# Scores of a unit in one PSUM bank, centring moved by two units, and scores moved ahead of the values, in a two-layer attention and FFN kernel

## The chip, the cores and the metric

The kernel runs on one core of a Trainium2 chip. The metric is the device time of one execution in microseconds. The median of three runs of the kernel before is 612.4 us.

## What is computed

Sixteen sequences of 128 tokens with 128 features pass two layers. Each layer is multi-query attention (16 heads of 64, one key and one value head, one null key in front, causal mask, key mask, bias), and after it a feed-forward part; the result is added to x. Layer 1's FFN is dense with ternary weights; layer 2's is a mixture of 8 experts, top 2, capacity 320.

```python
q = (ln(x) @ Wq).reshape(b, n, 16, 64)            # layer 1: l2norm(q), l2norm(k), times 8
k, v = split(ln(x) @ Wkv)                         # null key and value from cond_64 in front
sim = einsum(q, k) + bias                         # layer 1: bias from a small network
attn = softmax(where(causal | masked, -max, sim)) # layer 2: bias is an input, key mask
x = x + ffn(ln(einsum(attn, v) @ Wout, g_out))    # layer 2: routed experts
```

## The kernel before

All matmuls are in float32. The work is written engine by engine, with semaphores by hand. A batch is one sequence; `b` counts the 16 batches of a layer, `B` those of both layers, and `i` is `b % 2`. The 128 queries of a batch are cut into four units `u` of 32 queries; since the mask is causal, unit u needs only 33, 65, 97 or 129 keys (`WIDTH`, the null key included). Heads lie as four groups (h, e), so that one unit's scores are four blocks of 128 x WIDTH[u].

In this text layer 1 and layer 2 are the code's layer 0 and 1. Per batch of layer 2 the queues hold, in program order:

- TensorE (`attention_second`): scores of unit 0 (L855); transposes of unit 2's probabilities of the batch before (L873); values of the pair, units 0 and 1 of the batch before (L881, L882); scores of unit 1; transposes of unit 3 of the batch before; output projection of b - 2 (L910); scores of unit 2; values of units 2 and 3 (L891); input transpose (L801); scores of unit 3; transposes of the pair (L862, L864); keys and values (L819, L821) and queries (L828) of b + 2.
- VectorE: for each unit `biased` (L1547) reads the scores from PSUM, adds the masked bias and takes the maximum; `divide` (L1555, L1559) normalises the unit before; `outputs` (L1571) copies the values from `psO` to `OT`. In unit 0 then follow `centre` of b - 3 (L1608, L1610) and `input_norm` of b + 2 (L1498); in unit 1 `rescale` of b - 3 (L1615); in unit 2 the statistics and copy of the projection of b - 2 and `moments`; in unit 3 `variance` of b - 2 (L1604). `centre` and `rescale` exist from b = 3 on. Routing work stands in b = 10, 11, 14 and 15.
- ScalarE: exponentials (L1255) and the copies of the transposed probabilities to `PT` (L1268, L1262), of keys, queries and inputs.
- Pool: the four bias additions of the next batch (L630), the value subtraction (L613), and `output_rstd` (L577) of b - 2, which waits for `variance`.

Layer 1's queues interleave the same steps in another order; there unit 3 is read in the next batch, and ScalarE also takes squares of the queries for their norms (L1224).

The scores lie in `psS`, two PSUM banks of 512 columns. Head half h of every unit is in bank h. So the scores of a unit wait for the reads of all units before it (`scores_ready`, four for each unit):

```python
apart(pe, ..., (s["scores_ready"], 4 * n))
for h in range(2):
    m = pe.matmul(psS[:, h, 0:2 * w], qT[i][:, h, u].rearrange("p m q -> p (m q)"),
                  kk[i][:, :, 0:w], start=True, stop=True)
```

`over` unrolls the first and last batches of a layer and loops over the rest. `apart` issues waits, the values in registers where they depend on the loop.

Of the kernel before, what the change touches and what calls it, by code (L numbers as in the profile page):

```python
# [54 lines left out]
UNITS = P // QB  # L55
# [13 lines left out]
def build(nc, a, out):  # L69
    ctx = ExitStack()  # L70
    with ctx:
# [250 lines left out]

        def unit_psum(u):
            return psS[:, :, 0:2 * WIDTH[u]].rearrange("p h (e k) -> p h e k", e=2)

# [430 lines left out]
        def _(pe):  # L756
# [88 lines left out]
            def scores(layer, b, u, i):  # L845
                B = b + NB * layer
                n = 4 * B + u
                w = WIDTH[u]
                if no(b, 0) and u == 0:
                    pe.wait_ge(s["kk_null"], 4 * (layer + 1))  # L850

                apart(pe, *([(s["kk_ready"], B + 1), (s["q_ready"], 2 * B + 2)] if u == 0 else []),
                      (s["scores_ready"], 4 * n))
                for h in range(2):
                    m = pe.matmul(psS[:, h, 0:2 * w], qT[i][:, h, u].rearrange("p m q -> p (m q)"),  # L855
                                  kk[i][:, :, 0:w], start=True, stop=True)
# [136 lines left out]
            def attention_second():  # L993
                def batch(b, i):
# [3 lines left out]
                    for u in range(UNITS):  # L998
                        scores(1, b, u, i)
                        if u < 2 and not first:  # L1000
                            turn_probs(B - 1, u + 2, 1 - i)
                        if u == 0 and not first:
                            values_pair(B - 1, 1 - i)
                        if u == 1 and not first and not no(b, 1):
                            project(1, b - 2, i, not last)
# [411 lines left out]
        def _(dve):  # L1417
# [125 lines left out]
            def biased(n, u, i):  # L1543
                apart(dve, (s["probs_ready"], n - 3), (s["bias_ready"], n + 1), (s["scores_psum"], n + 1))
                for g in range(4):
                    h, e = g // 2, g % 2
                    dve.tensor_tensor_reduce(sc[u][:, h, e, :], unit_psum(u)[:, h, e, :], unit_masked(i, u)[:, h, e, :],  # L1547
                                             -1.0, -FAR, ALU.add, ALU.min,
                                             accum_out=negmax[:, u, g:g + 1]).then_inc(s["scores_ready"], 1)
# [201 lines left out]
            def attention_second():  # L1751
                def batch(b, i):
# [4 lines left out]
                    for u in range(UNITS):  # L1757
# [12 lines left out]
                        if u == 2 and not first and not no(b, 1):  # L1770
                            moments(B - 2, i)
                        if u == 0 and normed_now:
                            centre(b - 3, 1 - i)
                        if u == 0 and not last and not no(b, NB - 2):
                            input_norm(1, b + 2, i)
                        if u == 3 and not first and not no(b, 1):
                            variance(b - 2, i)
                        if u == 1 and normed_now:
                            rescale(b - 3, 1 - i)
# [249 lines left out]
```

## Time and profile before

| | |
|---|---|
| median of 3 runs | 612.4 us (610.82 to 613.22) |
| the profiled execution | 614.04 us, span 612.3 us |
| TensorE busy | 491.3 us (80%) |
| VectorE busy | 433.2 us (71%) |
| ScalarE busy | 377.9 us (62%) |
| Pool busy | 310.9 us (51%) |
| scores on TensorE, L855 | 512 instructions, 104.7 us |
| `biased` on VectorE, L1547 | 512, 93.6 us, idle before them 29.6 us |
| granted TensorE clock | mean 0.931 of full speed, 1.00 in most of both attention layers |

Layer 1's attention lies from about 21 to 216 us, the dense FFN to 285, layer 2's attention to about 480, the rest of the routing to 500, the experts to 577, and the gathering of the results behind. Busy time is that of one execution; matmul ends are modelled, so what a TensorE step costs is best read from start to start, where nothing is awaited. Behind a row, in brackets, stands the idle time of its engine before it and who ended it.

### The profile page before, as it was taken

To read this page: it belongs to the slowest core of one execution; us is meant where nothing else is said; L and a number is where in the kernel's file an instruction comes from. 1 tells how busy PE (TensorE), PEld (TensorE's weight loads), DVE (VectorE), ACT (ScalarE), POOL (GpSimd) and SP (SyncE) were. 2 spreads that over 40 slices of the span, in tenths; PEclk is the share of its full clock that TensorE was granted. 3 is DMA by queue.
4 is the path that set the end of the run, shared out by engine and by line. 5 is a ranking of instruction groups with operands and counts; after the bars stand their busy time and mean duration, and the time that the engine had idled before them with its cause. 6 is when DMAs were issued, how large, how long until landed. Compare 5 with 4: busy or idle time off the path is not lost.

```text
span 612.3 us, 13755 instructions
## 1 busy us (share of the span) xinstructions
PE 491.3 (80%) x3220; PEld 395.2 (65%) x3220; DVE 433.2 (71%) x2148; ACT 377.9 (62%) x1475; POOL 310.9 (51%) x368
## 2 busy tenths in 40 slices
PE   3678999999999877948898998988978419999920
PEld 1456777777777655647787887867756307878720
DVE  4899999999999775554778898899797603343403
ACT  1677898888888655634878778767775003443510
POOL 4576666655656517664433343344755531545560
PEclk9789999999999899978899999999998758999975
DMA  5450028331000000000021120000101021222117
GB/s 171 104 151 19 21 60 140 90 97 54 6 8 6 6 1 1 1 0 8 5 77 40 42 75 4 8 6 10 40 26 36 33 74 31 70 61 74 42 34 210
DMA packets 54696, 29.73 MB, mean 49 GB/s; under 512 B 19884, under 2 KB 51572, under 8 KB 54644
## 3 DMA queue, kind: packets, MB, share of 16 engines
q1 hardware_dynamic: 48900, 22.09, 14.6%
q0 software_dynamic: 2560, 4.90, 2.5%
q10 hardware_dynamic: 3184, 2.16, 1.1%
q8 instruction: 18, 0.29, 0.2%
q14 instruction: 34, 0.28, 0.2%
HBM read 16.13 MB, written 10.90 MB: 44 GB/s over the span
## 4 chain that ended last, share of the span: by engine, by line
PE 45%; DVE 20%; issue 14%; POOL 7%; DMA 5%; ACT 4%; SPq 1%; DVEq 1%; another core or an unknown queue 1%; ACTq 0%; POOLq 0%
PE psS L855 9%; PE psS L1152 5%; DVE sc L1547 5%; PE psA L910 4%; PE psO L891 4%; PE psQ L828 4%; PE psQ L812 3%; PE psQ L1142 3%; PE psT L873 2%; DVE centred L1610 2%; DVE OT L1571 2%; POOL wide_buf L630 2%; PE psA L1142 1%; PE psO L1142 1%; ACT qT L1238 1%
## 5 line engine op out<-in xcount | busy, mean ns | idle before, releaser
L1255 ACT ACTIVATE sc<-sc,negmax 128x97 f32<-128x97 f32 (+3 forms) x512 | 179.0, 354 | 34.0 <-DVE negmax L1547 32.2
L855 PE MATMUL psS<-kk,qT 128*128 128x194 f32 (+3 forms) x512 | 104.7, 327 | 23.9 <-DVE negmax L1547 22.2
L1547 DVE CUSTOM_DVE_ANT_0 sc<-psS,wide_buf 128x97 f32<-128x97 f32 (+3 forms) x512 | 93.6, 238 | 29.6 <-PE psS L855 26.6
L630 POOL TENSOR_TENSOR wide_buf<-bias,mask 128x132 f32<-128x132 f32 (+3 forms) x128 | 109.5, 881 | 9.8 <-DVE negmax L1547 4.2
L855 PEld LDWEIGHTS psS<-kk,qT 128*128 128x128 f32 x512 | 79.0, 195 | 50.3 <-issue 47.5
L1255 ACT ACTIVATION_READ_ACCUMULATOR sc<-sc,negmax 128x1 f32 x512 | 97.4, 190 | 0.0
L577 POOL TENSOR_TENSOR qrn<-qssc,half 128x9 f32<-128x9 f32 (+1 forms) x32 | 55.8, 1745 | 59.1 <-DVE qssc L1533 59.1
L1559 DVE TENSOR_TENSOR pn<-sc,rsum 128x128 f32<-128x128 f32 (+3 forms) x128 | 71.7, 560 | 6.8 <-DVE rsum L1555 0.2
L910 PE MATMUL psA<-Wo,OT 128*128 128x128 f32 (+1 forms) x512 | 65.2, 281 | 1.7 <-DVE OT L1571 1.7
L910 PEld LDWEIGHTS psA<-Wo,OT 128*128 128x128 f32 x512 | 62.1, 195 | 2.5 <-DVE OT L1571 2.5
L1571 DVE TENSOR_SCALAR OT<-psO,cols 128x512 f32<-128x512 f32 x64 | 47.6, 744 | 2.7 <-PE psO L891 1.8
L1268 ACT COPY PT<-psT 96x512 f32<-96x512 f32 x64 | 37.0, 577 | 15.8 <-PE psT L873 9.9
L873 PE MATMUL psT<-ident,pn 128*96 128x128 f32 (+1 forms) x256 | 39.6, 278 | 6.0 <-issue 4.1
L1547 DVE DVE_READ_ACCUMULATOR2_ANT negmax<- 128x1 f32 x512 | 41.6, 81 | 0.4 <-issue 0.2
L748 POOL DMA_INDIRECT choice_rows<-hT,tags x24 | 22.5, 939 | 37.1 <-ACT hT L1398 24.5
L891 PE MATMUL psO<-PT,vp 96*64 96x256 f32 (+1 forms) x256 | 34.8, 390 | 7.9 <-DVE OT L1571 4.3
L873 PEld LDWEIGHTS psT<-ident,pn 128*96 128x96 f32 (+1 forms) x256 | 28.5, 137 | 19.1 <-issue 18.5
L642 POOL DMA_INDIRECT slot_rows<-Y,dest_u x32 | 31.4, 980 | 18.1 <-issue 6.7
L812 PE MATMUL psQ<-Wq,xnT 128*128 128x512 f32 x64 | 36.7, 660 | 1.1
L1238 ACT ACTIVATE qT<-psQ 128x512 f32<-128x512 f32 x64 | 34.6, 586 | 4.5 <-PE psQ L841 4.1
L613 POOL TENSOR_TENSOR vp<-kvs,vnull 128x64 f32<-128x64 f32 x32 | 12.9, 403 | 47.2 <-PE psO L891 47.1
L828 PE MATMUL psQ<-xnT,Wq 128*128 128x128 f32 x256 | 32.9, 284 | 0.0
(298 smaller groups left out, 1004.1 us busy)
## 6 DMA issues: line engine op xcount, KB each, us to landing
slot_rows<-empty SPq DMA_DIRECT2D x2, 1390.0 KB, 9.7
xb<-slot_rows SPq DMA_DIRECT2D x16, 139.0 KB
vp_u<-vp SPq DMA_DIRECT2D x128, 8.0 KB, 1.7
choice_rows<-zero_row SPq DMA_DIRECT2D x8, 256.0 KB, 3.0
wide_buf<-choice_rows SPq DMA_DIRECT2D x8, 256.0 KB, 4.7
vp_u<-vp SPq DMA_DIRECT2D x64, 16.0 KB, 1.8
eW<-in_L_ffn_W SPq DMA_DIRECT2D x4, 256.0 KB, 3.0
gT<-in_L_ffn_W SPq DMA_DIRECT2D x4, 256.0 KB, 3.2
```

The source lines that it names most:

```text
L577: pool.tensor_tensor(dst, src, half[:, 0:k], ALU.pow).then_inc(done, count)
L630: pool.tensor_tensor(unit_masked(i, u).rearrange("p h e k -> p (h e) k"), unit_bias(layer, u).rearrange("p h e k -> p (h e) k"), mask[laye ...
L812: pe.matmul(psQ[:, h, :], xnT[i][:], Wq[0][:, 512 * h:512 * (h + 1)], start=True, stop=True).then_inc(s["q_psum"], 1)
L828: m = pe.matmul(psQ[:, h, j * P:(j + 1) * P], Wq[1][:, (4 * h + j) * P:(4 * h + j + 1) * P], xnT[i][:], start=True, stop=True)
L855: m = pe.matmul(psS[:, h, 0:2 * w], qT[i][:, h, u].rearrange("p m q -> p (m q)"), kk[i][:, :, 0:w], start=True, stop=True)
L873: m = pe.transpose(psT[0:k, probs_bank(u, i), g * P:(g + 1) * P], pn[u][:, g, :], ident[:])
L891: m = pe.matmul(psO[DH * e:DH * (e + 1), 2 * P * (u - 2):2 * P * (u - 1)], vp[i][0:k, :], PT[u - 1][0:k, :, e, :], start=True, stop=True)
L910: m = pe.matmul(psA[:, Y_AT[layer]:4 * P], OT[i][:, j].rearrange("p u q -> p (u q)"), Wo[layer][:, j, :], start=(j == 0), stop=(j == 7))
L1255: m = act.activation(v, v, ACT.Exp, bias=negmax[:, u, g:g + 1], scale=-1.0, accum_out=psum_row[:, u, g:g + 1])
L1547: dve.tensor_tensor_reduce(sc[u][:, h, e, :], unit_psum(u)[:, h, e, :], unit_masked(i, u)[:, h, e, :], -1.0, -FAR, ALU.add, ALU.min, accum ...
L1559: dve.tensor_tensor(pn[u][:], sc[u][:].rearrange("p h e k -> p (h e) k")[:, :, 1:k + 1], rsum[:, u, :].unsqueeze(2).broadcast_to([P, 4, k] ...
L1571: dve.tensor_scalar(OT[i][:, :, 2 * half_of:2 * half_of + 2, :], v, cols[:, C_VN:C_VN + 1], None, ALU.add).then_inc(s["out_ready"], 1)
```

## The change

`psS` is used by unit: units 0 and 2 lie whole in bank 0 and unit 1 in bank 1, with both head halves side by side; unit 3, whose 516 columns don't fit in one bank, has half 0 in bank 1 and half 1 in bank 0. The waits follow: unit 0 and 1 wait for the reads of the batch before, unit 2 for that of unit 0, the first half of unit 3 for that of unit 1, and its second half, by a wait of its own, for that of unit 2. This holds for both layers. In layer 2 the scores of unit 1 are issued before the values of the pair. On VectorE in layer 2 `centre` is issued in unit 2 behind `moments`, and `rescale` in unit 3 behind `variance`.

```diff
+        def score_bank(u, h):
+
+            w = WIDTH[u]
+            if u == UNITS - 1:
+                return psS[:, 1 - h, 0:2 * w]
+            return psS[:, u % 2, 2 * w * h:2 * w * (h + 1)]
...
-                      (s["scores_ready"], 4 * n))
+                      (s["scores_ready"], 4 * (n - u) if u < 2 else 4 * (n - 1)))
                 for h in range(2):
-                    m = pe.matmul(psS[:, h, 0:2 * w], qT[i][:, h, u].rearrange("p m q -> p (m q)"),
+                    if u == UNITS - 1 and h == 1:
+                        apart(pe, (s["scores_ready"], 4 * n))
+                    m = pe.matmul(score_bank(u, h), qT[i][:, h, u].rearrange("p m q -> p (m q)"),
...
                     for u in range(UNITS):
-                        scores(1, b, u, i)
-                        if u < 2 and not first:
-                            turn_probs(B - 1, u + 2, 1 - i)
+                        if u != 1:
+                            scores(1, b, u, i)
+                        if u == 0 and not first:
+                            turn_probs(B - 1, 2, 1 - i)
+                        if u == 0:
+                            scores(1, b, 1, i)
                         if u == 0 and not first:
                             values_pair(B - 1, 1 - i)
+                        if u == 1 and not first:
+                            turn_probs(B - 1, 3, 1 - i)
...
-                    dve.tensor_tensor_reduce(sc[u][:, h, e, :], unit_psum(u)[:, h, e, :], unit_masked(i, u)[:, h, e, :],
+                    dve.tensor_tensor_reduce(sc[u][:, h, e, :], score_bank(u, h)[:, e * WIDTH[u]:(e + 1) * WIDTH[u]],
+                                             unit_masked(i, u)[:, h, e, :],
...
-                        if u == 0 and normed_now:
-                            centre(b - 3, 1 - i)
                         if u == 0 and not last and not no(b, NB - 2):
                             input_norm(1, b + 2, i)
+                        if u == 2 and normed_now:
+                            centre(b - 3, 1 - i)
                         if u == 3 and not first and not no(b, 1):
                             variance(b - 2, i)
-                        if u == 1 and normed_now:
+                        if u == 3 and normed_now:
                             rescale(b - 3, 1 - i)
```

## Rows read from the trace of the kernel before

**Rows 1.** Stretches: from:to, us, each engine's busy us, TensorE clock, DMA.
```profile
317.10:396.80 79.70, 72.81 (x548) 63.61 (x547) 68.47 (x358) 63.88 (x281) 30.87 (x42) 1.00 0.14 39
306.73:317.10 10.37, 10.29 (x80) 8.90 (x79) 7.46 (x47) 8.66 (x39) 1.06 (x2) 1.00 0.19 58
396.80:422.23 25.43, 21.63 (x165) 18.32 (x164) 24.03 (x141) 18.46 (x82) 8.78 (x12) 1.00 0.03 6
422.23:445.17 22.94, 21.06 (x159) 18.27 (x157) 19.05 (x102) 17.33 (x76) 16.58 (x20) 1.00 0.11 32
445.17:458.04 12.87, 8.65 (x60) 6.84 (x58) 11.74 (x68) 8.88 (x42) 8.27 (x10) 1.00 0.10 29
...
76.69:146.18 69.49, 67.47 (x441) 51.65 (x439) 65.16 (x330) 60.19 (x259) 44.66 (x46) 1.00 0.40 89
```

**Rows 2.** Time line of TensorE, layer 2, b = 7: start us, us, instruction.
```profile
365.08 0.63 PE L873 MATMUL psT<-ident,pn 128*128 128x128 f32 x4 [0.15 <-issue]
365.55 2.02 PE L910 MATMUL psA<-Wo,OT 128*128 128x136 f32 x16
367.96 0.90 PE L855 MATMUL psS<-kk,qT 128*128 128x194 f32 x4 [0.40 <-DVE negmax L1547]
369.30 1.09 PE L891 MATMUL psO<-PT,vp 96*64 96x256 f32 x8 [0.44 <-DVE OT L1571]
```

**Rows 3.** Time line of TensorE, layer 2, b = 2.
```profile
309.76 2.02 PE L910 MATMUL psA<-Wo,OT 128*128 128x136 f32 x16
311.61 0.82 PE L855 MATMUL psS<-kk,qT 128*128 128x194 f32 x4
312.37 1.09 PE L891 MATMUL psO<-PT,vp 96*64 96x256 f32 x8
313.38 0.33 PE L801 MATMUL psA<-ident,xn 128*128 128x128 f32 x1
```

**Rows 4.** Time line of VectorE, layer 2, b = 7.
```profile
364.90 0.86 DVE L1608 SCALAR_TENSOR_TENSOR centred<-gate_sum,o_mv,Y 128x8 f32<-128x8 f32 x1
365.68 1.29 DVE L1610 SCALAR_TENSOR_TENSOR centred<-Y,o_mv,g_out 128x128 f32<-128x128 f32 x1
366.90 0.33 DVE L1498 TENSOR_SCALAR xn<-X,mv,rstd 128x128 f32 x1
...
371.75 0.29 DVE L1547 CUSTOM_DVE_ANT_0 sc<-psS,wide_buf 128x129 f32<-128x129 f32 x1 [0.79 <-PE psS L855]
```

**Rows 5.** Time line of Pool, layer 2, b = 7.
```profile
365.70 1.14 POOL L630 TENSOR_TENSOR wide_buf<-bias,mask 128x516 f32<-128x516 f32 x1
370.47 0.57 POOL L613 TENSOR_TENSOR vp<-kvs,vnull 128x64 f32<-128x64 f32 x1 [3.63 <-PE psO L891]
374.26 0.55 POOL L577 TENSOR_TENSOR o_rs<-o_ve,half 128x1 f32<-128x1 f32 x1 [3.22 <-DVE o_ve L1604]
```

**Rows 6.** Time line of VectorE, start of layer 2 and behind its last batch.
```profile
286.74 1.25 DVE L1498 TENSOR_SCALAR xn<-X,mv,rstd 128x128 f32<-128x128 f32 x1
...
482.57 0.22 DVE L1608 SCALAR_TENSOR_TENSOR centred<-gate_sum,o_mv,Y 128x8 f32<-128x8 f32 x1
482.71 0.34 DVE L1610 SCALAR_TENSOR_TENSOR centred<-Y,o_mv,g_out 128x128 f32<-128x128 f32 x1
```

**Rows 7.** Time line of TensorE, layer 1, b = 7.
```profile
117.53 1.09 PE L891 MATMUL psO<-PT,vp 96*64 96x256 f32 x8
118.73 1.11 PE L855 MATMUL psS<-kk,qT 128*128 128x258 f32 x4
119.67 0.27 PE L801 MATMUL psA<-ident,xn 128*128 128x128 f32 x1
```

**Rows 8.** Time lines: TensorE b = 0, VectorE b = 15, ScalarE behind it.
```profile
291.57 2.06 PE L855 MATMUL psS<-kk,qT 128*128 128x258 f32 x4 [1.01 <-DVE negmax L1547]
...
463.19 0.23 DVE L1547 CUSTOM_DVE_ANT_0 sc<-psS,wide_buf 128x65 f32<-128x65 f32 x1 [1.34 <-PE psS L855]
...
477.03 0.58 ACT L1268 COPY PT<-psT 128x512 f32<-128x512 f32 x1 [5.00 <-remote]
```

More of the change, by code:

```diff
@@ L321, in unit_masked @@
             return masked_bias[i][:, BIAS_AT[u]:BIAS_AT[u + 1]].rearrange("p (h e k) -> p h e k", h=2, e=2)
-        def unit_psum(u):
-            return psS[:, :, 0:2 * WIDTH[u]].rearrange("p h (e k) -> p h e k", e=2)
+        def score_bank(u, h):
[3 more added lines that the diff above has]
+            return psS[:, u % 2, 2 * w * h:2 * w * (h + 1)]
         def probs_bank(u, i):
```

## The prediction

> **What bounds the kernel now.** I read the stretches first, then the waits and time lines of one batch of each attention layer. In [rows 1] the reader should compare the first two lines. The first holds seven batches of layer 2, b = 3 to 9, in 79.70 us, so 11.39 us each, with TensorE busy 72.81 us (91%). The second is batch b = 2 of the same layer: 10.37 us, TensorE busy 10.29. It does the same TensorE work. What it lacks is `centre` and `rescale`, which start at b = 3, and almost all of the Pool work (1.06 us in it, 4.4 a batch later). So about 1 us a batch is stall, and its size is the difference of two rows.
>
> Where it stalls stands in [rows 2]: TensorE waits 0.15 us ahead of the transposes of unit 3, 0.40 ahead of the scores of unit 2 (for VectorE to have read those of unit 1), and 0.44 ahead of the values (for `OT` of the pair), together 0.99. Each of these is VectorE being late. Why it is late is in [rows 4]: after unit 0, `centre` takes from 364.90 to 366.90, 2.00 us, for one operation on 8 columns (0.86) and one on 128 (1.29). The same two take 0.22 and 0.34 late in the kernel [rows 6]. Their ends fall on the ends of Pool's bias additions: the first ends at 365.76, where Pool's last addition starts (365.70), and the second at 366.97, where that ends (366.84) [rows 4, 5]. Row L1498 of 1.25 us in [rows 6] beside others of 0.33 [rows 4] says that a tensor_scalar can be held in the same way. The Trainium skill has this as a lock (SBUF — State Buffer, "Who interferes with whom": a VectorE instruction with two SBUF inputs and a GpSimd instruction that reads SBUF block each other whole); the trace agrees, with 1.29 us against 0.34.
>
> In layer 1 TensorE and VectorE are both near full: 67.47 and 65.16 us of 69.49 [rows 1]. The values start at 117.53 and the scores of unit 3 at 118.73 [rows 7], 1.20 us later, where the values cost 1.01 (312.37 to 313.38 in [rows 3]). So 0.19 us is a stall on the old bank rule.
>
> **The change part by part.**
>
> *Centre to unit 2, rescale to unit 3 (layer 2, VectorE).* This takes 2.00 us out between unit 0 and unit 1, and puts the same two instructions behind `moments` in unit 2. There Pool has only the 0.57 us value subtraction at 370.47 and then nothing up to 374.26 [rows 5], and VectorE sits idle 0.79 us ahead of unit 3's scores [rows 4]. The price there: 0.14 + 0.34 = 0.48 us by the starts and lengths of [rows 6], inside the 0.79 idle: nothing. From the other side, if Pool holds them as now, 2.00 less 0.79, or 1.2 us a batch on the path. I take 0.5, since Pool's row there is one short operation. `rescale` moves 0.2 to 0.3 us from before the statistics to the end of the batch, where it is ahead of the read of V; TensorE works through the next batch's query projection then, so it hides. The semaphore of the square root, which Pool gives at the end of the batch before, is then long there; its wait costs nothing.
>
> What is late next: `input_norm` now stands at the spot where `centre` was, while Pool still adds biases. If it is held to the end of Pool's third addition (365.7) it costs 0.8 instead of 0.27, and it ends at about 366.0 rather than 367.2 (366.90 and 0.33): unit 1's scores, behind it, are read 1.2 us earlier than now. The page named above would hold it whole, as a tensor_scalar between two SBUF tiles; the sum below is the same with it. The stall ahead of unit 2's scores (0.40) goes in both cases, since those scores then follow the projection, which starts at 365.55 [rows 2] and takes 1.85 (309.76 to 311.61 in [rows 3]), and end by 368.2 with their read not yet awaited. The stall ahead of the values (0.44) goes as `OT` is 1.2 to 1.7 us earlier. The 0.15 ahead of unit 3's transposes stays: it hangs on the division of unit 3, which follows unit 0 as before; b = 2 has it too.
>
> *Two banks.* Unit 1 no longer waits for unit 0's read, unit 2 waits for unit 0 instead of unit 1, and the first half of unit 3 waits only for unit 1. Reads stay on another bank than writes. In layer 2 these waits are over by then in b = 2 already (unit 2's scores start 1.85 after the projection and the values 0.76 later, without a wait [rows 3]), so beyond what the centring gives I count nothing. In layer 1 the first half of unit 3 may start straight behind the values: 0.19 us a batch, over the 14 batches that have values in front: 2.7; half of unit 3's scores, 0.47 of 0.94 (118.73 to 119.67 [rows 7]), is the most that this rule can give back, or 6.6 in all. I take 2.2, as VectorE in that layer is 94% busy [rows 1] and part of the stall may pass to it. Added are two waits and a register computation a batch on TensorE's queue, and with the half wait a bubble if the read of unit 2 were late: it ends before the first half is through, so none. Lower bound: a loss of 0.1 a batch (3 us), as the matmul pair is split.
>
> *Unit 1's scores ahead of the pair's values.* Moves 0.54 us of scores 0.88 us earlier. It lets VectorE take unit 1 at once where it would wait; that is b = 15, where it now waits 1.34 us for them [rows 8] and where `centre` is cheap. The pair's values come 0.5 later, and so may `OT`; VectorE is then still in unit 1, so that hides. No DMA and no Pool instruction moves; SP's queue is untouched.
>
> **Sum.** A batch of layer 2 goes from 11.39 to 11.39 - 0.40 - 0.44 = 10.55; from the other side, b = 2 shows 10.37. I take 10.40, as in b = 2 the 0.15 ahead of unit 3 is contained.
> - b = 3 to 9: 7 x 0.99 = 6.9.
> - b = 10, 11: 25.43 us with VectorE busy 24.03 [rows 1]. VectorE itself is the bound (routing), so what it saves counts: 2.00 - 0.48 - about 0.2 for the held `input_norm` = 1.3 each, 2.6.
> - b = 12, 13: 22.94 less 2 x 10.4 = 2.1; I take 1.9.
> - b = 14: VectorE 11.74 of 12.87 busy; 1.1.
> - b = 15 and what hangs on it: 1.34 of wait, part of which returns at unit 3: 0.9.
> - b = 0 to 2: 0.6, from b = 0, where unit 3's scores wait 1.01 us for VectorE [rows 8], and half of them no longer would.
> - Layer 1: 2.2.
> Together 16.2. The profiled execution took 614.04 us (span 612.3 and 1.7 around it), 0.3% over the median of 612.4; 16 off gives 598.0 there and 596.4 against the median. I forecast 596.5, and 592 to 600 as its own range.
>
> Behind attention nothing is changed, and I expect it to shift as a whole. One thing may take some back: ScalarE sits idle 5.00 us ahead of the last copy of probabilities [rows 8], some 2 us of it after the transposes it needs. If that is bound to something that doesn't shift, up to 2 us is lost.
>
> **The rivals.**
> - *Half the gain (603).* In b = 2 Pool was nearly idle, so 10.37 is a batch without contention. With Pool's additions moved against VectorE's division of unit 3 (0.95 when held) and `input_norm`, the transposes of unit 3 and through them the whole chain come 0.5 later: 11 batches x 0.5 = 5.5, and layer 1 gives 1 instead of 2.2: about 6.7 less, 603. For it: the held L1498 [rows 6]. Against: the division is already held in the batches that run at 11.39.
> - *Layer 1 gives the most (591).* If the loop there is closed by the read of unit 2 and not by the projection, 0.47 a batch is given back, 6.6 instead of 2.2: 592, and with 10.3 in layer 2, 591. Against: only 0.19 of stall is seen.
> - *The scores' order and banks do nothing (599).* Only the centring acts; 2.2 and 0.9 fall away, giving 599.5. This is the case of a change that doesn't do part of what it says.
> - *Slower (616).* The hold moves along: VectorE runs early, Pool's bias additions with it late, and `centre` in unit 2 is held for its 2.00 us again. Then unit 3's read comes 2.00 - 0.79 = 1.2 late, and with it the division of unit 2, the transposes of unit 2 and the first scores of the next batch. It decides where this 1.2 is over the 0.99 saved: 12 batches x 0.2 = 2.4, and 1.5 for the split wait, 616. Against it: Pool's additions end at 366.84 and can't start again before `variance` at the end of the batch [rows 5].
>
> The Trainium skill has a rule against banks shared in time (PSUM — Partial Sum Buffer, "PSUM bank collisions raise a hardware error"): engines may work at one time only in different banks. The change keeps to it, so by that page the overlap is free; no row of before shows scores written beside scores read.
>
> **How the numbers follow.** Forecast 0.62, half the gain 0.18, most of layer 1 0.06, centring alone 0.09, slower 0.03, and 0.02 for no change by a mix of these. The range reaches from 591.0 to 604.0, from the second rival's time to just past the first's; outside are the slower cases and a tail at either side. A measurement of this kernel can tell some 0.5%, or 3 us, from no change. Faster by more than that: 0.94; within: 0.03; slower: 0.03.
>
> **What would show it.** Layer 2's batches at 10.4 us with TensorE idle only ahead of unit 3's transposes; L1610 at 0.34 and L1608 at 0.22, beside an idle Pool; L1498 either at 0.33 or at 0.8; VectorE's idle time ahead of unit 3 shrunk from 0.79 to about 0.3. In layer 1 the scores of unit 3 start 1.01 behind the values, and the period falls from 11.58 (69.49 / 6 [rows 1]) to 11.4. I am wrong if L1610 is still over 1 us, if the wait for `OT` stays, or if a new wait stands ahead of the second half of unit 3.

## The result

The changed kernel takes 597.33 us (median of 4 runs, 595.6 to 598.9) beside 611.61 us of the kernel before on the same chip (4 runs, 610.7 to 613.2): ratio 0.976, 95% interval 0.972 to 0.979. That is 14.3 us of gain where 16.2 were forecast, and the time lies 0.8 us from the forecast of 596.5. The total was right. Not all of its terms were, as the trace shows.

The profiled execution took 598.86 us with a span of 597.1. The stretches of [rows 1], in the trace of after (from:to, us, each engine's busy us, TensorE clock, DMA; b = 3 to 9, 10 to 11, 12 to 13 and 14 of layer 2):

```profile
314.00:387.03 73.03, 70.91 (x549) 61.26 (x548) 63.34 (x357) 63.29 (x280) 31.98 (x42) 1.00 0.16 43
387.03:413.77 26.74, 22.60 (x166) 19.72 (x165) 22.59 (x139) 17.78 (x78) 8.11 (x12) 0.94 0.03 6
413.77:434.78 21.01, 20.06 (x159) 17.63 (x158) 19.24 (x104) 16.95 (x77) 16.72 (x20) 1.00 0.11 31
434.78:446.66 11.88, 7.95 (x60) 6.47 (x58) 10.40 (x67) 9.34 (x44) 8.21 (x10) 0.98 0.12 38
```

Seven batches fell from 79.70 to 73.03 us, and TensorE is now busy for 97% of them, where it was 91%. The second line did not fall: 26.74 where 25.43 stood, and it is the only one with a granted clock well below full, 0.94.

TensorE in b = 7 of layer 2, against [rows 2]:

```profile
357.95 0.63 PE L879 MATMUL psT<-ident,pn 128*128 128x128 f32 x4
358.42 2.02 PE L916 MATMUL psA<-Wo,OT 128*128 128x136 f32 x16
360.27 0.82 PE L861 MATMUL psS<-kk,qT 128*128 128x194 f32 x4
361.02 1.09 PE L897 MATMUL psO<-PT,vp 96*64 96x256 f32 x8
```

All three waits of [rows 2] are gone, also the 0.15 us ahead of unit 3's transposes, which the prediction had left standing. The starts (1.85 and 0.75 apart) are those of b = 2 in [rows 3]. VectorE and Pool in the same batch, against [rows 4, 5]:

```profile
356.99 0.86 DVE L1571 TENSOR_TENSOR pn<-sc,rsum 128x512 f32<-128x512 f32 x1
357.77 0.92 DVE L1509 TENSOR_SCALAR xn<-X,mv,rstd 128x128 f32 x1
...
362.63 0.19 DVE L1620 SCALAR_TENSOR_TENSOR centred<-gate_sum,o_mv,Y 128x8 f32<-128x8 f32 x1
362.75 0.34 DVE L1622 SCALAR_TENSOR_TENSOR centred<-Y,o_mv,g_out 128x128 f32<-128x128 f32 x1
363.42 0.29 DVE L1558 CUSTOM_DVE_ANT_0 sc<-psS,wide_buf 128x129 f32<-128x129 f32 x1 [0.33 <-PE psS L861]
```
```profile
356.25 3.45 POOL L634 TENSOR_TENSOR wide_buf<-bias,mask 128x132 f32<-128x132 f32 x4
362.20 0.60 POOL L617 TENSOR_TENSOR vp<-kvs,vnull 128x64 f32<-128x64 f32 x1 [2.50 <-PE psO L897]
```

`centre` costs 0.19 and 0.34 us where it cost 0.86 and 1.29, and VectorE's idle time ahead of unit 3 is 0.33 where it was 0.79. `input_norm`, now the operation that stands inside Pool's four additions (356.25 to 359.70), costs 0.92 where it cost 0.33. The hold has moved along, to an operation that pays less for it. (To be held means here that an operation of VectorE takes longer than it does beside an idle Pool.)

### The profile page after: what moved, and what is told of

It is laid out like the page before. It is cut to its first block, busy times and chain, and to the rows that moved or that the text cites. A ratio compares the mean times of both kernels' runs of the same rounds, so it can differ in the third digit from the quotient of the medians.

```text
span 597.1 us, 13780 instructions
## 1 busy us (share of the span) xinstructions
PE 487.9 (82%) x3220; PEld 393.3 (66%) x3220; DVE 425.6 (71%) x2148; ACT 377.0 (63%) x1475; POOL 312.2 (52%) x368
## 4 chain that ended last, share of the span: by engine, by line
PE 58%; DVE 12%; issue 12%; POOL 6%; ACT 5%; DMA 4%; another core or an unknown queue 1%; SPq 1%; DVEq 0%; ACTq 0%; POOLq 0%
PE psS L861 11%; PE psA L916 7%; PE psS L1163 6%; PE psT L879 4%; PE psQ L816 4%; PE psO L897 4%; PE psQ L832 4%; PE psQ L1153 3%; PE psO L887 2%; PE psO L888 2%; DVE sc L1558 2%; POOL wide_buf L634 2%; ACT sc L1266 2%; PE psO L1153 1%; PE psA L1153 1%
## 5 line engine op out<-in xcount | busy, mean ns | idle before, releaser
L861 PE MATMUL psS<-kk,qT 128*128 128x194 f32 (+3 forms) x512 | 103.2, 323 | 11.1 <-DVE negmax L1558 11.0
L916 PE MATMUL psA<-Wo,OT 128*128 128x128 f32 (+1 forms) x512 | 67.2, 287 | 1.4 <-DVE OT L1583 1.4
L916 PEld LDWEIGHTS psA<-Wo,OT 128*128 128x128 f32 x512 | 64.0, 199 | 2.3 <-DVE OT L1583 2.2
L617 POOL TENSOR_TENSOR vp<-kvs,vnull 128x64 f32<-128x64 f32 x32 | 13.9, 434 | 42.4 <-PE psO L897 42.3
```

The source lines that it names most:

```text
L861: m = pe.matmul(score_bank(u, h), qT[i][:, h, u].rearrange("p m q -> p (m q)"), kk[i][:, :, 0:w], start=True, stop=True)
L916: m = pe.matmul(psA[:, Y_AT[layer]:4 * P], OT[i][:, j].rearrange("p u q -> p (u q)"), Wo[layer][:, j, :], start=(j == 0), stop=(j == 7))
```

## What each stretch gave

A stretch here runs from the first scores of one batch to those of another, read off TensorE's time line of each profile, in us. "L1" is the loop of layer 1 (b = 4 to 9 of it in brackets), "between" the time from its last batch to the first of layer 2, "rest" what follows the first scores of b = 15. Changed 2 and 3 are the changed kernel measured again, twice, at later times.

```
              L1      (b4-9)  between  b0-2   b3-9   b10-11 b12-13 b14    rest
before        181.20  69.49   79.06    31.92  79.70  25.43  22.94  12.87  154.26
after         180.36  68.71   77.84    31.31  73.03  26.74  21.01  11.88  150.46
changed 2     179.75  68.71   79.69    31.34  73.03  26.74  22.32  10.83  149.80
changed 3     179.99  68.78   78.85    31.32  73.02  24.70  21.80  10.84  150.03
centring      181.71  69.50   77.86    31.81  72.74  26.85  21.62  10.47  150.73
banks         180.40  68.71   79.61    31.39  79.20  25.34  22.84  12.04  150.92
no order      179.71  68.70   81.59    31.31  73.79  24.70  21.13  10.79  154.04
short adds    181.33  69.49   77.70    31.71  71.56  22.98  20.92  11.55  155.62
warm          179.56  68.71   78.79    31.32  73.03  25.72  21.92  11.38  153.91
project first 180.58  68.70   81.63    31.07  75.27  25.29  20.91  10.83  151.24
no split      180.89  69.48   81.01    32.18  72.73  26.84  21.67  11.07  150.75
gated         180.10  68.71   81.66    33.22  71.25  23.37  21.51  15.43  150.63
gated, warm   179.74  68.72   78.95    32.12  71.23  23.36  21.51  15.70  153.65
```

Three columns are poor evidence for any part. "Between" spreads over 77.7 to 81.7 and "rest" over 149.8 to 155.6 with no relation to the edits. The spread of "L1" comes from its first two batches, which take 14.2 to 16.6 and 11.1 to 12.4 us in kernels that are alike there. From b = 2 on, layer 1's loop takes 154.07 us before and 152.84, 152.85 and 153.00 in the three profiles of the changed kernel. In contrast, b = 3 to 9 take 73.03, 73.03 and 73.02 there. So the parts are judged by such stretches, and the whole by medians, which tell differences of about 3 us and no less.

A sum of seven batches can still mislead. One by one, b = 3 to 9 take, in us:

```
              b3     b4     b5     b6     b7     b8     b9
before        11.22  11.48  11.39  11.42  11.39  11.41  11.39
after         10.11  10.97  10.19  10.32  10.19  11.06  10.19
centring      10.21  11.05  10.28  10.32  10.28  10.32  10.28
banks         11.12  11.34  11.29  11.41  11.29  11.46  11.29
no order      10.10  10.97  10.19  11.08  10.19  11.07  10.19
no split      10.20  11.05  10.28  10.32  10.28  10.33  10.27
```

## The experiments

**Centring alone.** The kernel before, with `centre` and `rescale` moved as in the change, and the old banks and order.

```diff
-                        if u == 0 and normed_now:
-                            centre(b - 3, 1 - i)
...
+                        if u == 2 and normed_now:
+                            centre(b - 3, 1 - i)
...
-                        if u == 1 and normed_now:
+                        if u == 3 and normed_now:
                             rescale(b - 3, 1 - i)
```

> The kernel before, with the centring and rescaling of layer 2 moved to units 2 and 3 and nothing else. My theory: the centring is most of the change, since it is no longer held behind Pool's bias additions. It gives about 11 us of the 14 (ratio 0.981 to 0.984), b = 3 to 9 take 10.3 to 10.5 us each instead of 11.39, and L1610 takes 0.34. Rival (the bank rule is what frees TensorE): the waits of unit 2 for VectorE's read of unit 1 stay, and the gain is under 6 us (ratio over 0.990).

Measured: 601.81 us beside 614.09, ratio 0.982 (0.976 to 0.988). The seven batches take 72.74 us: this part alone gives the whole of their gain. Layer 1 stays at 69.50.

**Banks and waits alone.** The kernel before with `score_bank` and its waits, in the old order.

```diff
-                      (s["scores_ready"], 4 * n))
+                      (s["scores_ready"], 4 * (n - u) if u < 2 else 4 * (n - 1)))
                 for h in range(2):
...
+                    if u == UNITS - 1 and h == 1:
+                        apart(pe, (s["scores_ready"], 4 * n))
```

> The kernel before, with the scores' banks alternating by unit and their waits, but the centring and the order on TensorE as before. My theory: layer 1 gains 1.3 us over its 16 batches and 1.2 behind them, layer 2 next to nothing, since its waits follow from VectorE being late; together 2 to 4 us (ratio 0.993 to 0.997). Rival (bank rule): 8 us or more (ratio under 0.988).

Measured: 606.13 beside 614.09, ratio 0.988 (0.982 to 0.993). Of these 8 us the loops account for 1.2 (layer 1 from b = 2), 0.5 (b = 0 to 2), 0.5 (b = 3 to 9), 0.2 and 0.8 (b = 10 to 14), 3.2 in all. The rest lies in the spread of medians and in the tail, 150.92 in its profile and 154.26 in that of before; it can't be put down to the banks.

**The order taken back.** The changed kernel with unit 1's scores again behind the values of the pair.

```diff
-                        if u != 1:
-                            scores(1, b, u, i)
...
-                        if u == 0:
-                            scores(1, b, 1, i)
+                        scores(1, b, u, i)
...
```

> The changed kernel with unit 1's scores back behind the values of the pair. My theory: b = 3 to 9 run as in the changed kernel or up to 0.1 us a batch slower; in b = 11 and b = 15 the idle time of TensorE is cut in two by unit 1's scores less than before, the clock falls all the same. Time within 1.5 us of the changed kernel's 597.3 (ratio 0.975 to 0.980). Rival (the order carries part of the gain): over 3 us slower than the changed kernel.

Measured: 603.12, ratio 0.982 (0.977 to 0.988). The seven batches lose 0.76 us, and all of it in one, b = 6 (11.08 where after has 10.32); the other six agree with after to 0.01 us. There the division of unit 3 is held (1.46 us where after has 0.69). So unit 1's scores ahead of the values give an ordinary batch nothing, and only one more batch is held without them. b = 11 took 13.02 us with the clock at full, not the low clock that was expected. The higher total is "between" and "rest" (81.59 and 154.04).

**Pool's additions made short.** The kernel before, where Pool adds only the first column of each bias in layer 2 from the third sequence on. The other columns keep old values; all work of the other engines stays.

```diff
-                k = WIDTH[u]
+                k = WIDTH[u] if layer == 0 or no(b, 0) or no(b, 1) else 1
...
```

> The kernel before, but in layer 2 from its third sequence on Pool adds bias and mask for the first column of each block only, so those scores get stale bias values in the other columns; the rest is computed. The centring stays where it was, in unit 0. My theory (the two instructions are held by Pool's additions): L1608 takes 0.22 and L1610 0.34 us there, without moving, and b = 3 to 9 take about 10.4 us. Rival (the instructions are slow for another reason, such as their place or their operands): L1610 stays near 1.29 and the batches near 11.4 us.

Measured: 598.38, ratio 0.975 (0.968 to 0.983). `centre` stands where it stood before the change. VectorE's groups in b = 3 to 9 (line, operation, shapes, count; busy us, mean ns), first of the kernel before, then of this one:

```profile
L1610 DVE SCALAR_TENSOR_TENSOR centred<-Y,o_mv,g_out 128x128 f32<-128x128 f32 x7 | 8.1, 1156 | 0.0
L1559 DVE TENSOR_TENSOR pn<-sc,rsum 128x512 f32<-128x512 f32 x7 | 6.4, 910 | 0.5
L1608 DVE SCALAR_TENSOR_TENSOR centred<-gate_sum,o_mv,Y 128x8 f32<-128x8 f32 x7 | 6.3, 893 | 0.0
```
```profile
L1559 DVE TENSOR_TENSOR pn<-sc,rsum 128x512 f32<-128x512 f32 x7 | 4.8, 692 | 0.5
L1610 DVE SCALAR_TENSOR_TENSOR centred<-Y,o_mv,g_out 128x128 f32<-128x128 f32 x7 | 2.4, 346 | 0.0
L1498 DVE TENSOR_SCALAR xn<-X,mv,rstd 128x128 f32 x6 | 2.0, 341 | 0.0
L1608 DVE SCALAR_TENSOR_TENSOR centred<-gate_sum,o_mv,Y 128x8 f32<-128x8 f32 x7 | 1.5, 221 | 0.0
```

So it is Pool's additions, and not the place in the batch, that made `centre` long. The batches take 71.56 us, less than in the changed kernel (73.03). The difference is what is still held there, by this view of after:

```profile
L1571 DVE TENSOR_TENSOR pn<-sc,rsum 128x512 f32<-128x512 f32 x7 | 6.6, 946 | 0.5
L1509 DVE TENSOR_SCALAR xn<-X,mv,rstd 128x128 f32 x6 | 6.0, 997 | 0.0
```

**The changed kernel again**, to see how far one kernel's time and stretches move.

> The changed kernel again, beside the next three on the same chip. A ratio of 0.973 to 0.980 to the kernel before. The batch b = 11 of layer 2 takes about 15 us with TensorE at a granted clock near 0.65 behind its gap; if it is near 13 in this profile, that loss is of single executions and not of the kernel.

Measured: 601.58 us (6 runs) beside 612.51 (11), ratio 0.981 (0.976 to 0.986). The seven batches, and b = 10 and 11, come out as in after, to 0.01 us. The ratio lies just above the range that was expected.

**TensorE kept busy.** In b = 10 and 11 the changed kernel lost where 2.6 us of gain was forecast. TensorE in b = 11 of after (time line, then two stretches of it):

```profile
404.17 0.63 PE L879 MATMUL psT<-ident,pn 128*128 128x128 f32 x4 [2.90 <-issue]
404.64 3.27 PE L916 MATMUL psA<-Wo,OT 128*128 128x136 f32 x16
407.70 1.29 PE L861 MATMUL psS<-kk,qT 128*128 128x194 f32 x4
```
```profile
404.17:405.20 1.03, 1.03 (x9) 1.03 (x10) 1.00 (x11) 0.51 (x3) 0.00 (x0) 1.00 0.00 0
405.30:408.60 3.30, 3.30 (x15) 3.30 (x15) 1.18 (x4) 2.42 (x11) 0.00 (x0) 0.50 0.00 0
```

TensorE idles for 2.90 us and works for 1.0 us at full clock. Then the granted clock is 0.50, the level of 1.2 GHz, up to about 408.6, and the projection takes 3.06 us from its start to that of the next scores, where it takes 1.85 at full clock [rows 3]. The experiment puts 24 idle transposes into that gap, and 24 ahead of the first scores of b = 15, where after idles for 2.83 us.

```diff
+                        if u == 0 and last:
+                            for _ in range(24):
+                                pe.transpose(psT[:, i, 0:P], ident[:], ident[:])
...
+                        if u == 1 and no(b, NB - 5):
+                            pe.wait_ge(s["probsT_ready"], 3 * (B - 1) + 1)
+                            for _ in range(24):
+                                pe.transpose(psT[:, probs_bank(3, 1 - i), 0:P], ident[:], ident[:])
```

> The changed kernel with 24 idle transposes of the identity (about 2.6 us of TensorE work, results unused) where TensorE has its two long gaps in layer 2: ahead of unit 3's transposes in b = 11 (2.90 us idle) and ahead of unit 0's scores in b = 15 (2.83 us idle). My theory: the clock falls because TensorE stood idle there, so kept busy it stays at 1.00, the projection of b = 11 takes 1.85 instead of 3.06 us from start to start, b = 11 takes about 13.2 us instead of 15.06, and the first steps of b = 15 are halved; 2 to 4 us faster than the changed kernel. Rival (the fall of the clock has another cause, or the added work delays what follows): b = 11 stays at 15 us or longer and the time is the same or up to 2 us more.

Measured: 600.46 beside 612.51, ratio 0.980 (0.976 to 0.984). TensorE and the clock in b = 11:

```profile
404.45 0.63 PE L879 MATMUL psT<-ident,pn 128*128 128x128 f32 x4 [0.30 <-issue]
404.92 2.02 PE L916 MATMUL psA<-Wo,OT 128*128 128x136 f32 x16
406.78 0.82 PE L861 MATMUL psS<-kk,qT 128*128 128x194 f32 x4
```
```profile
404.20:407.70 3.50, 3.15 (x24) 2.88 (x24) 2.53 (x15) 2.98 (x15) 0.00 (x0) 1.00 0.00 0
```

The clock stays at 1.00, the projection is back at 1.86 us, and b = 11 takes 14.04 instead of 15.06 us. In b = 15 the first scores take 0.40 from start to start (446.29 to 446.69) instead of 0.88 (446.64 to 447.52, clock 0.50). So the clock's part is some 1 us in b = 11. In b = 15 it is more: unit 2's scores start 5.49 us behind the first ones instead of 7.92. None of this last gain arrives. ScalarE then idles 6.73 us ahead of its last copy of probabilities, where it idles 3.46 in after, and the last scatter starts 37.33 us behind the first scores, against 37.40. The total doesn't show the rest either: 600.46, and 601.58 of the changed kernel beside it, are within the spread.

**The projection ahead of unit 3's transposes.** This lets TensorE work while it would wait for unit 3's division, and puts ScalarE's copy of those probabilities behind unit 1's exponentials.

```diff
-                        if u == 1 and not first:
-                            turn_probs(B - 1, 3, 1 - i)
                         if u == 1 and not first and not no(b, 1):
                             project(1, b - 2, i, not last)
+                        if u == 1 and not first:
+                            turn_probs(B - 1, 3, 1 - i)
...
```

> The changed kernel with the output projection of layer 2 issued ahead of unit 3's transposes on TensorE, and on ScalarE the copy of these behind the exponentials of unit 1. The projection's inputs are long ready, so it fills the wait for the division of unit 3. My theory (that wait is what is left of TensorE's idle time): b = 3 to 9 take 10.05 to 10.15 us each with none at 11, b = 11 has a gap of about 1 us and full clock, 13 us; 4 to 6 us faster than the changed kernel. Rival: the values now wait for ScalarE's later copy, the batches stay at 10.2 to 10.4, and the time is within 1.5 us of the changed kernel's.

Measured: 601.37, ratio 0.980 (0.976 to 0.984), and 75.27 us for the seven batches, 2.2 more than the changed kernel. Three batches take 10.28 and four (b = 3, 4, 6 and 8) 11.04 to 11.17. In the long ones the values wait for ScalarE; this is b = 6:

```profile
356.77 1.09 PE L897 MATMUL psO<-PT,vp 96*64 96x256 f32 x8 [0.94 <-ACT PT L1279]
```

In b = 6 the division is held to 1.25 us, so the copy behind it is late too: the wait for the division was traded for one for the copy. b = 11 took 13.41 us, at full clock.

**Unit 3 not split.** Both halves of unit 3 wait for the read of unit 2.

```diff
-                      (s["scores_ready"], 4 * (n - u) if u < 2 else 4 * (n - 1)))
+                      (s["scores_ready"], 4 * (n - u) if u < 2 else 4 * (n - 1) if u == 2 else 4 * n))
                 for h in range(2):
-                    if u == UNITS - 1 and h == 1:
-                        apart(pe, (s["scores_ready"], 4 * n))
```

> The changed kernel, but both halves of unit 3's scores wait for the read of unit 2, as one wait. My theory: in layer 2 nothing changes; in layer 1 the scores of unit 3 start about 0.15 us later behind the values, and its batches go back from about 11.45 to 11.55 us: 1 to 2 us slower than the changed kernel. Rival (the half wait is the main gain of the banks in layer 1): batches of 11.8 us or more; other rival (it does nothing): batches as in the changed kernel.

Measured: 602.84, ratio 0.983 (0.978 to 0.988). Six batches of layer 1 take 69.48 us, as before the change; with the split they take 68.70 to 68.78. From b = 2 to the end of the layer's loop it is 154.04, against 154.07 before and 152.84 to 153.00 in the changed kernel. So all of the gain in layer 1 is the half wait. In its trace and in that of after, layer 1, b = 7:

```profile
117.16 1.09 PE L895 MATMUL psO<-PT,vp 96*64 96x256 f32 x8
118.36 1.11 PE L859 MATMUL psS<-kk,qT 128*128 128x258 f32 x4
```
```profile
116.90 1.09 PE L897 MATMUL psO<-PT,vp 96*64 96x256 f32 x8
117.92 1.14 PE L861 MATMUL psS<-kk,qT 128*128 128x258 f32 x4
```

1.20 us with the whole wait, as in [rows 7], and 1.02 with the half. In layer 2 the split gives 0.9 in b = 0 to 2, and 0.1 in four of the seven batches b = 3 to 9 (10.19 against 10.28, say). The sum is lower without it (72.73), since b = 8 is not held there and takes 10.33 instead of 11.06.

**The changed kernel, a third time**, beside the next two.

> The changed kernel a third time, as the neighbour of the next two on the same chip. Ratio 0.973 to 0.983; b = 3 to 9 at 73.0 us and b = 11 at about 15.06 again.

Measured: 598.17 (6 runs) beside 612.04 (11), ratio 0.979 (0.976 to 0.981). Here b = 11 took 13.01 us where two profiles of the same kernel have 15.06. VectorE up to unit 3's division in b = 11, and Pool's additions beside it, in after and then here:

```profile
400.53 0.46 DVE L1883 TENSOR_TENSOR share<-top,lsum 128x14 f32<-128x14 f32 x1
401.03 0.59 DVE L1885 TENSOR_SCALAR base<-topf 128x14 f32<-128x14 f32 x1
...
402.27 0.19 DVE L1558 CUSTOM_DVE_ANT_0 sc<-psS,wide_buf 128x33 f32<-128x33 f32 x1 [0.40 <-issue]
...
402.95 1.12 DVE L1571 TENSOR_TENSOR pn<-sc,rsum 128x512 f32<-128x512 f32 x1
400.53 2.99 POOL L634 TENSOR_TENSOR wide_buf<-bias,mask 128x132 f32<-128x132 f32 x4
```
```profile
402.16 0.18 DVE L1883 TENSOR_TENSOR share<-top,lsum 128x14 f32<-128x14 f32 x1
402.37 0.29 DVE L1885 TENSOR_SCALAR base<-topf 128x14 f32<-128x14 f32 x1
...
403.32 0.19 DVE L1558 CUSTOM_DVE_ANT_0 sc<-psS,wide_buf 128x33 f32<-128x33 f32 x1 [0.40 <-POOL wide_buf L634]
...
404.00 0.69 DVE L1571 TENSOR_TENSOR pn<-sc,rsum 128x512 f32<-128x512 f32 x1
402.17 3.52 POOL L634 TENSOR_TENSOR wide_buf<-bias,mask 128x132 f32<-128x132 f32 x4
```

From `share` to the end of the division it is 3.54 us in after and 2.53 here: the same instructions, held by 1.0 us more in one execution than in the other. Pool's four additions go the other way, 2.99 and 3.52 us. In both, `share` and Pool's first addition start within 0.01 us of each other. Where `share` took 0.46 us, Pool had the way; where it took 0.18, VectorE had. TensorE's gap follows, 2.90 and 1.89 us, and in b = 11 only the longer one is followed by the low clock:

```profile
404.79 0.63 PE L879 MATMUL psT<-ident,pn 128*128 128x128 f32 x4 [1.89 <-issue]
```

The length of a gap alone doesn't decide that. In b = 15 of this profile TensorE idles 1.96 us, and from 447.80 the clock is at 0.50:

```profile
447.80:451.20 3.40, 3.40 (x24) 3.02 (x23) 3.19 (x24) 1.46 (x9) 2.21 (x3) 0.50 0.18 53
```

Changed 2 has the same gap of 1.96 us there, with the clock at 1.00 for the 5 us behind it.

**Pool's additions behind `input_norm`.** If `input_norm` and unit 3's division are what is still held, Pool has to start after them.

```diff
                     if not no(b, NB - 1):
+                        if not no(b, NB - 2):
+                            apart(pool, (s["xn_ready"], b + NB + 3))
                         for u in range(UNITS):
                             mask_bias(1, b + 1, u, 1 - i)
```

> The changed kernel, with Pool's four bias additions of layer 2 started only when input_norm of that batch is done (a wait on xn_ready), so that they can't hold the division of unit 3 and input_norm. My theory (what is left of the holds is what costs b = 4 and b = 8 their 0.8 us and lengthens the gap of b = 11): L1571 with 512 columns takes 0.69 in place of 0.95 us, L1509 0.34 in place of 1.0, b = 3 to 9 take 70.7 to 71.6 us in place of 73.03, none over 10.4, and b = 11 is 1 to 2 us shorter; 3 to 5 us faster than the changed kernel. Rival (the hold moves once more, to unit 0's division and through it to OT, and the values wait): b = 3 to 9 at 73 us or more, the time the same or slower.

Measured: 602.12 beside 612.04, ratio 0.983 (0.980 to 0.986), so not better than the changed kernel beside it. In the loop the reason holds: 71.25 us, lower than in any kernel above that does the whole work. VectorE's groups there:

```profile
L1573 DVE TENSOR_TENSOR pn<-sc,rsum 128x128 f32<-128x128 f32 x7 | 5.0, 717 | 0.9
L1573 DVE TENSOR_TENSOR pn<-sc,rsum 128x512 f32<-128x512 f32 x7 | 4.9, 693 | 0.5
...
L1511 DVE TENSOR_SCALAR xn<-X,mv,rstd 128x128 f32 x6 | 2.0, 342 | 0.0
```

`input_norm` and unit 3's division are free, and the division of unit 0 (128 columns) pays instead, 0.72 where it took 0.35. It is given back at both ends of the loop. In b = 14 `input_norm` isn't there and the wait neither, and VectorE's division and Pool's additions meet (VectorE, then Pool):

```profile
439.39 3.00 DVE L1573 TENSOR_TENSOR pn<-sc,rsum 128x512 f32<-128x512 f32 x1
```
```profile
438.87 2.97 POOL L634 TENSOR_TENSOR wide_buf<-bias,mask 128x132 f32<-128x132 f32 x4
```

The division takes 3.00 us: it starts during Pool's second addition and ends 0.55 behind the fourth. TensorE idles 3.73 us, the clock falls to 0.50 behind that, and the batch takes 15.43, where the changed kernel takes 10.83 to 11.88. In b = 0 the additions start 2.0 us behind the first scores (289.13) instead of 0.3 ahead of them (282.40 in after). They meet the dense layer's last update, which takes 2.03 us instead of 1.14, and the batch takes 12.84 instead of 11.10.

**The same with TensorE kept busy** in b = 11 (12 transposes) and b = 15 (24, as above).

> e9_gated with idle transposes of the identity on TensorE, 12 ahead of unit 3's transposes in b = 11 and 24 ahead of unit 0's scores in b = 15. My theory: the clock stays at 1.00 in both, the first steps of b = 15 are halved (0.4 in place of 0.86 us for unit 0's scores from start to start); 1 to 2 us faster than e9_gated in the profile's stretches, hardly to be told apart in the median. Rival: no difference, if the gaps of e9_gated are short enough to leave the clock alone.

Measured: 601.71, ratio 0.983 (0.980 to 0.986). No stretch changes by more than 0.4 us but b = 0 to 2, "between" and "rest". b = 0 took 11.85 us here, with the same gate and the same held update; 12.84 was partly a longer stretch of low clock (the query projection took 3.62 us there and 2.86 here). b = 11 had no low clock to mend. No version tried beats the changed kernel.

## Why the prediction was right, and where it wasn't

**The main term held.** For b = 3 to 9 the forecast was 6.9, the trace says 6.7 (79.70 to 73.03), and the other two profiles of the changed kernel the same. The reason given, VectorE late because `centre` stood in Pool's additions, is shown from two sides: taking `centre` out gives 72.74, and making Pool's additions short gives 71.56 with `centre` in its place. That the mean of a batch fits so well (10.40 forecast, 10.43 measured) is partly luck. Five batches take 10.10 to 10.32, less than forecast, and b = 4 and 8, where unit 3's division is held, take 11.0. `input_norm` was forecast at 0.33 or 0.8; its own end time in the forecast (366.0, from 364.90) would have given 1.1, and it came at 0.92 to 1.16. It cost little: with `input_norm` free, the gated kernel's b = 5, 7 and 9 take 10.02 where after takes 10.19, and b = 6 takes 10.32 in both.

**What holds the division in one batch and not in the next.** The forecast had no term for it. Unit 3's division and Pool's third addition start almost together. Here they are, first in b = 6 of after, then in b = 8:

```profile
346.97 0.69 DVE L1571 TENSOR_TENSOR pn<-sc,rsum 128x512 f32<-128x512 f32 x1
346.97 1.44 POOL L634 TENSOR_TENSOR wide_buf<-bias,mask 128x388 f32<-128x388 f32 x1
```
```profile
367.48 1.43 DVE L1571 TENSOR_TENSOR pn<-sc,rsum 128x512 f32<-128x512 f32 x1
367.46 0.90 POOL L634 TENSOR_TENSOR wide_buf<-bias,mask 128x388 f32<-128x388 f32 x1
```

Whoever is first has its usual time (0.69 the division, 0.90 the addition), and the other one pays. In b = 8 Pool is first by 0.02 us, and TensorE waits for it:

```profile
369.01 0.63 PE L879 MATMUL psT<-ident,pn 128*128 128x128 f32 x4 [0.92 <-issue]
```

With the centring alone or without the split Pool's addition starts 0.08 us behind the division in b = 8, and the division takes 0.69 there. With banks alone Pool is again first in b = 8, by 0.01, and the division takes 1.44. So the half wait, which comes with Pool's additions 0.09 us earlier, gains 0.1 in some batches and loses 0.7 in this one. At a distance under 0.01 us it can fall either way: in b = 6 VectorE is ahead by less than that in after and with the order taken back alike, and the division took 0.69 in the first and 1.46 in the second.

The rule quoted from the Trainium skill (SBUF — State Buffer, "Who interferes with whom") is borne out for `centre` and `input_norm`: with no Pool work beside them they are at 0.34, with it at about 1.

**The small terms.** b = 12 and 13: 1.9 forecast, 1.9 in after and 0.6 and 1.1 in the other two profiles, so the match in after is luck. b = 14: 1.1 forecast, 1.0 to 2.0. b = 0 to 2: 0.6 and 0.6, all from the half wait. The order: nothing was counted for it but its share in b = 15, and an ordinary batch gains nothing by it.

**Layer 1 was sized too high.** The step that failed was the 0.19 us of stall times 14, rounded down to 2.2. The stall does go (1.20 to 1.02), but the period falls by 0.13, from 11.58 to 11.45, and the loop from b = 2 on by 1.1 to 1.2 us. VectorE was 94% busy there [rows 1] and is 95% busy after (65.11 of 68.70 us). That it keeps the rest is likely and was not tested; the prediction named it and took off too little.

**b = 10 and 11 were wrong.** 2.6 us of gain was forecast since VectorE was taken as the bound. The step that failed is that what VectorE saves counts there in full. Its busy time fell by 1.44 us (24.03 to 22.59), and the two batches gained only 0.7 in the one profile without a low clock (25.43 to 24.70) and lost 1.3 in the two with it. What is last ahead of unit 3's transposes is its division, behind the read of unit 0, and that stands inside Pool's additions. `centre`, which was taken out, stood behind it: work taken from VectorE there doesn't bring the division nearer.

From the first scores of b = 11 to those transposes it is 4.3 us in the kernel before (408.92 to 413.23) and with banks alone, 4.4 to 4.5 in no order, gated and the third profile, and 5.5 in centring, no split, warm, and the other two profiles of the changed kernel. So two outcomes lie 1.0 us apart, with either order of the scores. The near tie of `share` with Pool's first addition came with the move of `rescale`, which now stands ahead of `share`. In the kernel before and with banks alone `share` starts 0.20 us ahead of Pool and takes 0.17. In every profile with `rescale` moved and Pool not gated the two start within 0.01 us; `share` takes 0.46 or more in six of them and 0.18 in two. Gated, Pool is away and it takes 0.17. No run moves `rescale` alone, so this is read from the traces and not tested; the prediction said of this move that it hides.

In each of the 5.5 us cases TensorE stood still for 2.2 us or more, and, unless the gap was filled, the clock fell behind it and cost about 1.6 us (1.2 at the projection, 0.4 at the scores). The filled kernel agrees: its b = 11 is 1.0 us longer than the third profile's, by the hold, and 1.0 shorter than after's; of the clock's 1.6 us, 0.46 stands in both as a wait for ScalarE's copy of the queries, which the slower projection hides.

**What made the total fit.** The span fell by 15.2 us. The loops of both layers give 9.7 of it (0.84 + 0.61 + 6.67 - 1.31 + 1.93 + 0.99) where 15.3 were forecast for them; with layer 1 counted from b = 2 they give 10.1. The rest, 1.2 "between", 3.8 in "rest" and 0.5 ahead of the first scores, lies where 0.9 was forecast. "Rest" holds at most about 0.6 that can be followed to the change, up to the last scatter; the 3 us behind it are of the size by which executions of one kernel differ. That the first measurement came within 1 us of the forecast is therefore partly luck.

The prediction's doubt about ScalarE's last copy stays open. Its idle time ahead of that copy shrank from 5.00 [rows 8] to 3.46, but in the warm, gated and no-order kernels it is 6.73, 6.41 and 6.04, and the 2.4 us that TensorE gained in b = 15 of the warm kernel were lost there. What ends that wait the profile doesn't show.

In three measurements the changed kernel's median was 14.3, 10.9 and 13.9 us below that of before, and its loops 9.7, 10.1 and 12.4 by the profiles. The value of the change is thus 11 to 14 us by the medians: 16.2 was 2 to 5 too high, and the first measurement lay at the favourable end.

**The rivals.** "Half the gain" (603) described the held division in b = 4 and 8 and layer 1 at 1 us rightly, but charged 0.5 us in all 11 batches, where 2 of 7 pay some 0.7. "Layer 1 gives most" falls by 69.49 to 68.71. "Centring alone" (599) is near: centring is all of the gain in b = 3 to 9, and the banks alone give 3.2 us in the loops. "Slower" needed `centre` held again in unit 2; it took 0.34.

## What to carry to other kernels

Before an operation is moved, list what the other engine that shares its memory does at the old and at the new place: the hold doesn't vanish, it goes to whoever stands there next, and the gain is the difference of the two prices. Look for pairs that start within some 0.02 us of each other: which of them pays can change with an unrelated edit, or from one execution to the next. An engine at 94% busy is a bound only if its work lies ahead of the wait that counts; follow the last wait, not the share. Judge a small part by stretches that repeat to 0.01 us, not by medians that scatter by 2 us, and look at them batch by batch: 0.76 us over seven batches was one batch.

## What the runs showed of the hardware

- Beside Pool's additions the operation that started first kept its time, and the other paid. The 512-column division took 0.69 us when it started with Pool's third addition (346.97), which then took 1.44; it took 1.43 when Pool started 0.02 us ahead, and the addition 0.90. In b = 14 of the gated kernel the division began during Pool's second addition and ended only behind the fourth, 3.00 us. Why it didn't get in between them isn't settled.
- TensorE writing scores in one bank while VectorE reads the other cost VectorE's reads nothing that can be seen: the reads of 33 columns take 193 ns on average in both kernels, and the same in after for those 56 of 128 that have a score matmul beside them. In before no read has one.
- A gap of 2.90 us in TensorE's work was followed by 3.4 us at a granted clock of 0.50, which began 1.1 us after the work did; one of 2.83 us by 6.8 us at 0.50. Behind one of 1.89 us the clock stayed at 1.00. Of three of 1.96 us in b = 15 (changed 2, changed 3 and no order), the last two were followed by 3.4 us at 0.50 and the first by none. Filling the gap with idle transposes kept the clock at 1.00 in both places, and on this kernel gave nothing that a median shows.
